# A Mamba layer and a mixture of experts on one core: the weights' pieces gathered in the last block, a norm one step earlier, and another order after the last block

## What is computed

```python
x_and_res = x @ W_in.T                        # 256 -> 2*512
xp, res = jnp.split(x_and_res, 2, axis=-1)
xc = silu(causal_conv(xp, conv_w) + conv_b)   # 4 taps, each channel by itself
ssm = xc @ W_x.T                              # B, C (16 states each) and dt
dt = softplus(dt @ W_dt.T + b_dt)
h = exp(A * dt_t) * h + dt_t * B_t * x_t      # over time, 512 channels, 16 states
y_t = (h * C_t).sum(states) + D * x_t
x = layernorm(x + silu(y + res) @ W_out.T)
w, e = top_k(softmax(x @ router_w.T), 2)      # w then divided by its sum
out = gelu(x @ w1[e].T + b1[e]) @ w2[e].T + b2[e]
x = layernorm(x + (out * w).sum(over the two))
```

## Time and profile before

| | |
|---|---|
| median of 3 runs | 1429.03 us (1427.63 to 1429.11) |
| the profiled execution's own time | 1429.47 us, its span 1427.7 us |
| Mamba blocks 0 to 7, by DVE's first and last scan | about 44 to 855 us |
| from there to the first expert matmul | 855 to 911 us |
| 71 expert slots, then the last stage | 911 to 1398 us, then to 1427.7 us |
| busy over the span | PE 90%, DVE 77%, ACT 70%, POOL 74% |

### The profile page before, as it was taken

How to read it: one execution, slowest core, us unless ns; L and a number is a source line. 1 busy time by engine, 2 the same in 40 slices (tenths; PEclk the granted TensorE clock), 3 DMA queues, 4 the chain that set the end, 5 groups by cost and what they waited for, 6 DMA issues and landing times. The chain is left out here.

```text
span 1427.7 us, 28835 instructions
## 1 busy us (share of the span) xinstructions
PE 1288.1 (90%) x8807; PEld 1090.3 (76%) x8808; DVE 1104.4 (77%) x1836; ACT 993.4 (70%) x1364; POOL 1052.6 (74%) x920
## 2 busy tenths in 40 slices
PE   6799899999998998998997996499999999999991
PEld 2468687787777787877886885499999999999981
DVE  6879999899899899899898896665665665665554
ACT  6899998999988999988988963334433433433434
POOL 3589798798998989998989997455555555555544
PEclk8799999999999999999999998699999999999995
DMA  8523141132331332331322327424465723522216
GB/s 280 173 79 97 61 122 63 56 120 79 101 108 68 99 103 71 105 104 64 109 82 75 111 85 246 152 42 107 123 160 144 206 41 74 140 41 37 34 20 243
DMA packets 91017, 150.75 MB, mean 106 GB/s; under 512 B 10892, under 2 KB 43276, under 8 KB 90928
## 3 DMA queue, kind: packets, MB, share of 16 engines
q1 hardware_dynamic: 73216, 121.24, 26.4%
q0 software_dynamic: 16704, 27.29, 9.5%
q10 hardware_dynamic: 1008, 1.07, 0.3%
HBM read 100.79 MB, written 48.78 MB: 105 GB/s over the span
## 5 line engine op out<-in xcount | busy, mean ns | idle before, releaser
L1448 POOL TENSOR_TENSOR arena<-arena 128x1024 f32<-128x1024 f32 x252 | 598.5, 2388 | 16.5 <-DVE arena L1107 10.1
L492 PE MATMUL d_ps<-ident,arena 128*128 128x128 f32 x2048 | 320.7, 280 | 44.2 <-DVE arena L1107 36.7
L492 PEld LDWEIGHTS d_ps<-ident,arena 128*128 128x128 f32 x2048 | 240.9, 143 | 150.4 <-DVE arena L1107 73.1
L1107 DVE TENSOR_TENSOR_SCAN arena<-arena,carry,d_ps 128x512 f32<-128x512 f32 x256 | 314.5, 1264 | 28.5 <-PE d_ps L492 21.5
L793 ACT ACTIVATE arena<-u_tok,b_tok 128x512 f32<-128x512 f32 x508 | 324.5, 711 | 6.5 <-PE d_ps L492 5.1
L1107 DVE TENSOR_TENSOR_SCAN arena<-arena,d_ps 128x512 f32<-128x512 f32 x256 | 301.2, 1207 | 30.1 <-PE d_ps L492 19.7
L505 PE MATMUL y_ps<-ident,arena 128*128 128x128 f32 x2048 | 297.3, 274 | 6.8 <-POOL arena L1448 5.5
L1796 ACT ACTIVATE h_t<-ht_ps 128x512 f32<-128x512 f32 x142 | 84.4, 594 | 284.0 <-PE ht_ps L1851 284.0
L807 ACT ACTIVATE arena<-dt,neg_a 128x2048 f32<-128x2048 f32 x127 | 253.1, 1993 | 2.3 <-DVE arena L1107 2.1
L505 PEld LDWEIGHTS y_ps<-ident,arena 128*128 128x128 f32 x2048 | 238.0, 142 | 9.5 <-POOL arena L1448 6.6
L1836 PE MATMUL h_ps<-arena,xg_t 128*128 x852 | 218.1, 405 | 1.3 <-DVE xg_t L1928 1.3
(11 more groups left out here) (230 smaller groups left out, 1552.7 us busy)
## 6 DMA issues: line engine op xcount, KB each, us to landing
arena<-c_rows SPq DMA_DIRECT2D x128, 256.0 KB, 3.3
arena<-weight_parts SPq DMA_DIRECT2D x20, 1024.0 KB, 5.5
weight_parts<-arena SPq DMA_DIRECT2D x64, 256.0 KB, 3.6
xg<-expert_rows POOLq DMA_DIRECT2D x71, 130.0 KB, 2.4
arena<-in_pieces SPq DMA_DIRECT2D x16, 512.0 KB, 8.9
arena<-in_pieces SPq DMA_DIRECT2D x64, 128.0 KB, 3.3
expert_out<-arena SPq DMA_DIRECT2D x1, 4224.0 KB, 15.2
weight_parts<-arena SPq DMA_DIRECT2D x4, 1024.0 KB, 4.6
```

The costliest lines, as they stand in the source:

```text
L492: last = nc.tensor.matmul(d_ps[:, c % 2, j * P:(j + 1) * P], ub[:, g % U_RING, j, c * P:(c + 1) * P], t.ident[:], start=True, stop=True, i ...
L1107: nc.vector.tensor_tensor_scan(h[:, g % H_RING, c, :], decay[:, g % D_RING, c, :], d_ps[:, c % 2, :], 0.0 if i % 2 == 0 else carry[:, n, c ...
L1448: nc.gpsimd.tensor_tensor(h[:, g % H_RING, lo:hi, :], h[:, g % H_RING, lo:hi, :], c_row[:, g % C_RING:g % C_RING + 1, :].broadcast_to([P, ...
```

## The change

Three things change.

1. **Pieces.** Step 1 is no longer a piece's step in blocks 0 to 6, which leaves seven in each of them (steps 3, 4, 6, 7, 9, 10, 12), and the last block splits fifteen, one in each step from 0 to 14.
2. **Norm.** In blocks 1 to 6 ACT's `normed()` stands at the end of its step 13, behind `ut_out(0)` and ahead of `ut_out(1)`, instead of at the end of step 14. In the last block it stays at step 12.
3. **After the last block.** On DVE `copy_group(2)` comes ahead of `router_place`, the first `own_low` comes behind the four norms, and the third to fifth come behind `tables()`. On POOL the reciprocal roots of groups 1 to 3 are made behind the second transfer of rows, with no transfers between them.

```diff
-        PIECE_STEPS = (1, 3, 4, 6, 7, 9, 10, 12)
+        PIECE_STEPS = (3, 4, 6, 7, 9, 10, 12)
+        LAST_STEPS = (0, 1, 2, 3, 4, 5, 6, 7, 8, 9, 10, 11, 12, 13, 14)
...
-            if n in PIECE_STEPS and 0 <= i < BLOCKS:
+            if i == BLOCKS - 1 and n in LAST_STEPS:
+                return len(PIECE_STEPS) * i + LAST_STEPS.index(n)
+            if n in PIECE_STEPS and 0 <= i < BLOCKS - 1:
                 return len(PIECE_STEPS) * i + PIECE_STEPS.index(n)
...
-                    if back and n == (12 if i == BLOCKS - 1 else 14):
+                    if back and n == (12 if i == BLOCKS - 1 else 13):
                         normed()
...
+                    copy_group(2)
                     router_place()
-                    own_low(0)
-                    copy_group(2)
                     add_group(0)
...
                     norm_group(3)
+                    own_low(0)
                     own_low(1)
-                    own_low(2)
                     router_pick(r)
-                    own_low(3)
-                    own_low(4)
...
-            for m in range(5, W_RING * W_LOADS):
+            for m in range(2, W_RING * W_LOADS):
                 own_low(m)
...
                     send_rows(p, 0)
-                    for j in range(TT):
+                    rstd_group(0)
+                    send_rows(p, 1)
+                    for j in range(1, TT):
                         rstd_group(j)
-                        send_rows(p, j + 1)
-                    for m in range(TT + 1, TT * TOPK):
+                    for m in range(2, TT * TOPK):
                         send_rows(p, m)
```

More of the change, by code:

```diff
@@ L306, in mamba @@
         zeros = h[:, ZERO_SLOT, 0, 0:DIM]
-        PIECE_STEPS = (1, 3, 4, 6, 7, 9, 10, 12)
+        PIECE_STEPS = (3, 4, 6, 7, 9, 10, 12)
+        LAST_STEPS = (0, 1, 2, 3, 4, 5, 6, 7, 8, 9, 10, 11, 12, 13, 14)
         PARTED = (EXPERTS - W_RING - 1) * PIECES
-        assert len(PIECE_STEPS) * BLOCKS == PARTED
+        assert len(PIECE_STEPS) * (BLOCKS - 1) + len(LAST_STEPS) == PARTED
         def piece_of(i, n):
-            if n in PIECE_STEPS and 0 <= i < BLOCKS:
+            if i == BLOCKS - 1 and n in LAST_STEPS:
+                return len(PIECE_STEPS) * i + LAST_STEPS.index(n)
+            if n in PIECE_STEPS and 0 <= i < BLOCKS - 1:
                 return len(PIECE_STEPS) * i + PIECE_STEPS.index(n)
```

## The result

| | before | changed |
|---|---|---|
| median | 1429.07 us (1427.63 to 1431.31, 4 runs) | 1451.32 us (1448.34 to 1452.75, 4 runs) |
| profiled execution, its span | 1429.47, 1427.7 us | 1451.35, 1449.7 us |

The ratio is 1.0152, with a 95% interval of 1.0131 to 1.0172: 1.5% slower, 22 us. The forecast was 1451.2 us.

What follows compares the result with a forecast made beforehand. POOL was taken to bound the last block, DVE blocks 1 to 6, with ACT setting the pace at two places. -11.0 + 3.5 + 20.7 + 6.9 + 2 + 0 = +22.1 us gave 1451.2 us; range 1438 to 1462.

Steps and rivals of the forecast that it cites:

- Norm and piece of step 1: Blocks 0 to 6: 2.0 us saved at each of five turns, 1.0 in block 0; -11.0 us in all.
- POOL's own work: Last block: five more `low_part`s ahead of POOL's step 13, 0.69 us each; +3.5 us.
- The added wait: Last block, steps 2 to 12: POOL waits 2.0 us for each late piece; +20.7 us after small corrections.
- S: Start of POOL's step in the last block, from which load, fetch and cast times are counted.
- The end of the block: Last block from POOL's step 13: cast of step 14 delays the second copy, logits and scans; +6.9 us.
- the clock: End of the last block: PE, idle some 4 us before the logits, then runs mostly at 1.2 GHz; +2 us.
- After the last block: Reordered DVE and POOL work after the last block: 0 us, bounds -2 and +3.
- (a): Rival, last block: the transfer is hidden and only seven `low_part`s are paid; 1423 us, 5%.
- (b): Rival, earlier blocks: they gain nothing, since POOL or PE takes over from ACT; 1462 us, 10%.
- (c): Rival, last block: the waits for pieces are half as long; 1438 us, 4%.
- (d): Rival, no change: early blocks gain their upper bound and the waits are half; 1431 us, 2%.

Runs made afterwards that it cites:

- e2: The kernel before with only the pieces' edit (seven in each of blocks 0 to 6, fifteen in the last), norm and tail as before: 1459.53 us, ratio 1.0209.
- e9: The changed kernel with DVE's second `y_u` product two scans later in blocks 1, 3 and 5: 1450.69 us, ratio 1.0142.
- e3: The changed kernel with SP's fetch and store ahead of `load_c` in the last block: 1425.49 us, ratio 0.9974.
- e4: The changed kernel with three buffers for pieces in place of two: 1427.42 us, ratio 0.9984.
- e10: The changed kernel with `load_c`'s wait kept ahead of the fetch in the last block, but its transfer issued behind the fetch: 1434.63 us, ratio 1.0040.
- e7: The kernel before with the norm's edit and the tail's order, pieces as before: 1415.12 us, ratio 0.9905.
- e11: The kernel before with the tail's order alone (DVE's and POOL's work after the last block): 1427.23 us, ratio 0.9986.
- e8: e3 with, besides, ACT's cast of piece 14 behind the second copy of the turned rows: 1420.55 us, ratio 0.9932.
- e1: The kernel before with only the norm's edit, pieces and tail as before: 1415.33 us, ratio 0.9907.

## Why the prediction was right, and where its terms were not

The mechanism was the one forecast, each link at its place, and the total (+22.2 us at `last_products`, forecast +22.1) is right to 0.1 us. That closeness is luck in part: three terms were off and cancelled.

- **Norm and piece of step 1, -11.0.** ACT's silu of block 7 came 11.25 us earlier, 9.6 of it in blocks 1 to 7 (forecast 10.0). The sum is right and its split is wrong. The link from the norm to DVE is as forecast: at the five turns DVE's wait for the pre-activation went from 1.9 to 2.4 us down to 0.2 to 0.6, some 9 us in all (forecast 8.5), and its wait for decays stayed. But the norm alone won 12.95 us: the turns 3 to 4 and 5 to 6 won 4.1 and 3.9, the other three 1.4 to 1.8. The piece of step 1 is worth nothing without the norm (e2), not 0.31 us a turn, and with it the seven pieces cost 3.4. The step that failed took all turns for alike and ACT for the only thing that makes DVE late: in two of the five turns DVE's `y_u` also meets POOL's products in a way that the change moves. That is shown for half of the 3.4 us (e9); the rest stays open. The 1.0 us of block 0 can't be told in a start-up that varies by 2.4.
- **POOL's own work, +3.5.** e3 shows 3.3. Right.
- **The added wait, +20.7.** It was 24.0, by the difference of the changed kernel and e3. The eleven waits of steps 2 to 12 that the forecast names add up to 23.6 (the twelfth of the 26.0, in step 13, lies in the end). S + 2.47, S + 2.90 and S + 6.74 are its S + 2.45, S + 2.88 and S + 6.65. Two small sizes failed: a wait is 2.2 us, not 2.0; and of the 1.9 us that POOL's small operations were to take off, step 8 took its 1.0 (a wait of 1.10) and the three others little (2.37, 1.96 and 2.07 us in steps 5, 11 and 12).
- **The end of the block, +6.9, and the clock, +2.** The end took 6.2 us more, both together. The cast of step 14 came at S + 9.4 and not at S + 10.3, since its fetch is the only one of the block with no `load_c` in front: 2.14 us to the cast in place of 3.36. The clock's term was 0. PE had stood idle for 8.1 us earlier, waiting for the norm behind the late cast of step 12, and ran at 0.50 then:

```profile
861.00:865.00 4.00, 2.63 (x13) 2.66 (x14) 0.65 (x1) 4.00 (x8) 4.00 (x3) 0.50 0.12 21
...
869.00:873.00 4.00, 2.55 (x25) 2.35 (x23) 2.29 (x3) 2.17 (x3) 3.14 (x4) 1.00 0.38 126
```

  By the logits it was back at 1.00, and PE's last idle time was 1.45 us, not 4. Where PE did idle 3.6 to 4.0 us right ahead of them (e3, e4, e10) the term was there: 1.7, 2.8 and 3.2 us.
- **After the last block, 0.** +0.55, the rest -0.8: within what these stretches vary by. The subtraction of the earlier trace rows took 0.24 us as forecast; POOL waited 2.47 us for the fourth group, five times what I thought. A slowing of POOL by the moved `own_low`s, which the prediction weighed, can't be seen in the time: e7 and e11 are no slower for the tail's order. POOL's timeline:

```profile
884.16 0.24 POOL L1522 TENSOR_TENSOR ex<-top 128x32 f32<-128x32 f32 x1
...
900.23 0.29 POOL L1551 TENSOR_SCALAR var<-mv 128x1 f32<-128x1 f32 x1 [2.47 <-DVE mv L1261]
```

- **The rivals.** (a), the hidden transfer, is not the changed kernel but is what e3 and e8 make of it: 1425.5 and 1420.6, forecast for it 1423. (b) fell: the early blocks gained. (c) rested on a landing of 2.3 us; it is what e10 comes near to (1434.6, forecast for it 1438). (d) needed both, larger gains and half the waits; neither came.

The Trainium skill (DMA: Bandwidth & Descriptors, Anatomy of one DMA — SWDGE (gpsimd) path) gives 2.0 us and the bytes at 436 GB/s for a transfer that GpSimd issues, by which I estimated 2.3 us for a piece. The pieces here are issued by SP. The landings of e10, 1.9 to 2.2 us, lie a little below that estimate; the 3.6 us of the changed kernel lie well above it, as each piece there stands behind a row of C.

The norm's edit without the pieces' beats both kernels: e1 (1415.3 us) and e7 (1415.1) are 14 us faster than before and 36 faster than the changed kernel.

## What to carry to other kernels

When work is added to a ring of buffers, count how many steps lie between a fetch and its use: here seven more pieces cost 3.3 us of work and 24 us of waits, because in consecutive steps the fetch lost its step to spare, and putting it ahead of the row load in the queue's list gave the 24 back with no more memory. Look what stands in front of a short transfer in its own queue, and what waits in order behind the operation that waits for it. Before a gain on one engine is multiplied by the number of blocks, see whether DVE's operations with two SBUF operands meet POOL's in some of them: here 3.4 of 13 us went in the two blocks with such a meeting, and moving DVE's product away gave about half of that back.

## What the hardware showed beyond that

- The same 128 KB from memory: 2.0 us from issue to landing (1.9 to 2.2) with no other transfer just ahead in the queue, 3.6 (3.4 to 4.1) with a row load issued 0.43 us before.
- A DVE product of two SBUF operands and a POOL product of 128x1024 ran one after the other wherever they met: DVE's 1.20 us became 2.89 or 2.95 when it came second, and when POOL was second its pair went from 4.68 to 5.72 us.
- TensorE's clock, after an idle time of 3.56 us: granted 0.50 in the 4 us that follow, 0.69 in the next. After 8.11 us of idle time, which ended at 862.37: 0.50 from 861 to 865, and 1.00 again from 869 on.
